# A feed-forward stage after attention: kept weights, inputs fetched during attention, VectorE's work in other pieces, and opening maxima in three buffers

## The reference

```python
x = x + 0.5 * ffn(layernorm(x), Wr, We)
x = x + attention(layernorm(x), Wq, bq, Wk, bk, Wv, bv, Wo, bo)   # 16 heads of 16, rotary q and k
x = x + 0.5 * ffn(layernorm(x), Wr, We)

def ffn(x, Wr, We):                      # 8 experts, each 256x256; both FFNs have the same weights
    logits = x @ Wr.T
    top_vals, top_idx = top_k(logits, 2); w = softmax(top_vals)
    # token t goes to its two experts if fewer than C = 1537 earlier picks of its sequence went there
    out[t] = sum over k of w[t, k] * (x[t] @ We[top_idx[t, k]]) if kept
```

## Time and profile before

| | us |
|---|---|
| median of 3 runs | 6634.64 (6630.81 to 6637.87) |
| profiled execution, its own time | 6634.04 |
| its span (profile) | 6632.2 |
| TensorE busy | 6263.3 (94%) |
| VectorE busy | 6035.8 (91%) |
| ScalarE busy | 4754.6 (72%) |
| GpSimd busy | 379.1 (6%) |

### The profile page before, as it was taken

One profiled execution on the slowest core, in us unless ns is written; L12 is line 12 of the kernel. 1 busy time (PEld: TensorE's weight loads), 2 busy tenths in 40 slices (PEclk: granted clock), 3 DMA queues, 4 the chain that ended last, 5 costly groups with the idle time before them and its releaser, 6 DMA issues. The chain is left out here.

```text
span 6632.2 us, 158232 instructions
## 1 busy us (share of the span) xinstructions
PE 6263.3 (94%) x54288; PEld 2797.8 (42%) x54288; DVE 6035.8 (91%) x6991; ACT 4754.6 (72%) x8698; POOL 379.1 (6%) x604
## 2 busy tenths in 40 slices
PE   7888579999999999999999999999999999996888
PEld 6666423333333333333333333333333333334666
DVE  7888579999999999999999999999999999963766
ACT  2222128888888888888888888888888888882111
POOL 2322300000000000000000000000000000001221
PEclk9999769999999999999999999999999999997999
DMA  2222301010100101010101010101010100001110
GB/s 80 93 91 94 89 10 16 13 16 13 16 17 13 19 10 19 10 19 10 19 10 23 10 22 14 16 13 16 13 16 13 17 16 13 3 3 66 42 47 25
DMA packets 120611, 177.08 MB, mean 27 GB/s; under 512 B 61616, under 2 KB 78784, under 8 KB 116800
## 3 DMA queue, kind: packets, MB, share of 16 engines
q1 hardware_dynamic: 120128, 169.43, 11.0%
HBM read 100.17 MB, written 69.21 MB: 26 GB/s over the span
## 5 line engine op out<-in xcount | busy, mean ns | idle before, releaser
L972 DVE TENSOR_REDUCE at_mx<-at_m 128x1 f32<-128x1024 f32 x4096 | 5008.5, 1224 | 117.3 <-PE at_m L849 97.0
L948 ACT ACTIVATE at_ex<-at_s 128x512 f32<-128x512 f32 x8192 | 4450.2, 595 | 754.9 <-PE at_s L870 185.7
L849 PE MATMUL at_m<-at_k,at_q 48*128 48x512 f32 x8192 | 3005.2, 449 | 63.4 <-DVE at_mx L972 50.0
L870 PE MATMUL at_s<-at_q,at_k 50*128 50x512 f32 x8192 | 2996.9, 444 | 0.0
L880 PE MATMUL at_po<-at_ex,at_v 128*32 128x256 f32 x32816 | 2624.5, 392 | 31.7 <-POOL at_v L818 31.7
L849 PEld LDWEIGHTS at_m<-at_k,at_q 48*128 48x128 f32 x8192 | 1214.7, 187 | 1769.5 <-DVE at_mx L972 1692.4
L880 PEld LDWEIGHTS at_po<-at_ex,at_v 128*32 128x32 f32 x32816 | 646.5, 108 | 1519.8 <-issue 748.1
L870 PEld LDWEIGHTS at_s<-at_q,at_k 50*128 50x128 f32 x8192 | 1211.8, 185 | 42.6 <-ACT at_ex L948 42.2
L272 PE MATMUL fr_ps<-fr_weh,fr_xl 128*128 128x512 f32 x512 | 179.5, 433 | 108.6 <-DVE fr_acc L443 108.6
L824 POOL COPY at_v<-at_vst 128x1024 f32<-128x1024 f32 x16 | 16.7, 1043 | 4598.1 <-DMA at_vst<-v_by_head 4283.5
L1202 PE MATMUL bk_ps<-bk_weh,bk_xl 128*128 128x512 f32 x512 | 172.3, 418 | 64.9 <-DVE bk_acc L1328 64.8
(11 more groups left out here) (167 smaller groups left out, 2664.9 us busy)
## 6 DMA issues: line engine op xcount, KB each, us to landing
at_q<-q_parts SPq DMA_DIRECT2D x96, 256.0 KB, 5.0
at_k<-k_parts SPq DMA_DIRECT2D x96, 256.0 KB, 6.3
q_parts<-fr_parts SPq DMA_DIRECT2D x64, 256.0 KB, 2.2
k_parts<-fr_parts SPq DMA_DIRECT2D x64, 256.0 KB, 2.4
attended<-at_o SPq DMA_DIRECT2D x256, 34.0 KB
fr_x<-in_x SPq DMA_DIRECT2D x16, 512.0 KB, 4.3
after_ffn<-fr_acc SPq DMA_DIRECT2D x16, 512.0 KB, 3.0
v_by_head<-fr_v SPq DMA_DIRECT2D x16, 512.0 KB, 4.1
```

Of the source, the lines that this page charges most:

```text
L849: ins = pe.matmul(pm[w][:, h * QB:(h + 1) * QB], Q[p][rows, base + i * P:base + (i + 1) * P], K[p][rows, c * CW + h * QB:c * CW + (h + 1) ...
L870: pe.matmul(ps[event(t) % NS][:, :], K[p][rows, j * P:(j + 1) * P], Q[p][rows, sb_ * QU + g * QB:sb_ * QU + (g + 1) * QB], start=True, sto ...
L948: ac.activation(Ex[QUAD * (j % NX) + 2 * g + 1 - half][:, :], ps[event(t) % NS][:, :], ACT.Exp)\
L972: ve.tensor_reduce(out=mx[u][:, i, c:c + 1], in_=pm[w][:, :], op=ALU.max, axis=AX.X)\
```

## The change

- Weights, their split parts and the constants of both FFNs (ident, wr, before, ones, order, weh, wel) are allocated around all three phases and made once, by front_phase. back_phase has no loads or splits of them.
- New tiles and semaphores (ahead_tiles) live through attention and back_phase. SyncE fills them in the last head pair: at its first unit the sums of sequence 0, three constants and the inputs of groups 0 and 1 (fetch_ahead), at its last unit the reciprocals (fetch_reciprocals_ahead). VectorE takes those of sequence 0 at the end of its work in attend_phase. The sums of sequence 1 are loaded at the start of back_phase and inverted in group 0.
- The opening maxima use three buffers (pm[0], pm[1] and two of the three banks of the scores), a whole chunk after the other. VectorE's first two units stand outside its loop, for the buffers' names.
- In back_phase the orders of TensorE and VectorE are others, at the start and in each group, and product 15 goes to bank 1.

```diff
-        ps = [ctx.enter_context(nc.psum_tensor(f"{name}_s{k}", [P, QB], F32)) for k in range(NS)]
+        s_all = ctx.enter_context(nc.psum_tensor(f"{name}_s", [P, NS * QB], F32))
+        ps = [s_all[:, k * QB:(k + 1) * QB] for k in range(NS)]
+        first = [pm[0], pm[1], s_all[:, 0:CW]]
+        FIRST = 2 * (STEPS + AHEAD)
...
+                        if not more and sb_ == 0:
+                            hold(sp, s_out, (2 + PB * SB) * (QUAD * DMA), s_tick)
+                            fetch(sp)
+                        if not more and sb_ == SB - 1:
+                            fetch_reciprocals(sp)
                         hold(sp, s_e, u * EVENTS + (EVENTS + COPY_AT + 1 + E0), s_tick)
...
+                def first_chunk(n):
+                    m, w = n // 2 % STEPS, n % 2
+                    i, c, base = m // CQ, m % CQ, n // RED * QU
+                    if n >= len(first):
+                        pe.wait_ge(s_mr, 2 + n - len(first) + 1)
+                    rows = slice(HALF * w, HALF * w + ROWS)
+                    for h in range(2):
+                        last = pe.matmul(first[n % len(first)][:, h * QB:(h + 1) * QB],
+                                         Q[0][rows, base + i * P:base + (i + 1) * P],
+                                         K[0][rows, c * CW + h * QB:c * CW + (h + 1) * QB], start=True, stop=True)
+                    last.then_inc(s_m, 1)
...
-                for m in range(STEPS + AHEAD):
-                    for half in (0, 2, 1, 3):
-                        max_chunk(m % STEPS, half, 0, m // STEPS * QU, m // STEPS)
+                for n in range(FIRST):
+                    first_chunk(n)
...
+                ve.wait_ge(ahead.s_sum, GB * DMA)
+                ve.reciprocal(ahead.recs[0][:, :], ahead.sums[0][:, :]).then_inc(ahead.s_all, 1)
...
+def fetch_ahead(sp, t, sources, constants):
+    attended, residual, _, sums, _ = sources
+    for src, dst in sums(t.sums[0], 0):                 # 8 pieces
+        sp.dma_start(dst, src).then_inc(t.s_sum, DMA)
+    for dst, src in zip((t.spread[:, :], t.wo[:, :, :], t.bo[:, :]), constants):
+        sp.dma_start(dst, src).then_inc(t.s_c, DMA)
+    for u in range(2):
+        for c in range(NC):
+            sp.dma_start(t.at[u][:, c, :], attended(u, c)).then_inc(t.s_at[u], DMA)
+        sp.dma_start(t.x[u][:, :, :], residual(u)).then_inc(t.s_x[u], DMA)
+
+def fetch_reciprocals_ahead(sp, t, sources, tick):
+    _, _, reciprocals, _, store = sources
+    hold(sp, t.s_all, 1, tick)
+    for dst, src in store(t.recs[0], 0):                # 8 pieces
+        sp.dma_start(dst, src).then_inc(t.s_rd, DMA)
+    hold(sp, t.s_rd, GB * DMA, tick)
+    for u in range(2):
+        sp.dma_start(t.rec[u][:, :], reciprocals(u)).then_inc(t.s_rec[u], DMA)
...
+    BANK = [n % NB for n in range(CHUNKS - 1)] + [1]
...
-                        if n == 0:
-                            need(pe, s_ac, g * STEPS)
+                        if n < 2:
+                            need(pe, s_ac, g * STEPS - (0 if n else EP * NB))
                         elif n >= NB:
-                            pe.wait_ge(s_ac, g * STEPS + EP * (n - NB + 1))
+                            last_use = max(m for m in range(n) if BANK[m] == BANK[n])
+                            pe.wait_ge(s_ac, g * STEPS + EP * (last_use + 1))
...
-                pe.wait_ge(s_c, 7 * DMA)
-                for n in range(2):
-                    spread_out(n, n, 0)
-                    project(n)
+                pe.wait_ge(s_c, 3 * DMA)
+                spread_out(0, 0, 0)
+                project(0)
                 turn(0)
+                spread_out(1, 1, 0)
                 router(0)
-                pe.wait_ge(s_wl, 1)
+                project(1)
                 positions(0)
```

More of the change, by code:

```diff
@@ L103, in sem @@
             return nc.alloc_semaphore(f"{name}_{n}")
[L105 to L108, removed]
+        ident, wr, before, ones, order, weh, wel = shared
+        before32, keep = sb("before32", [P, P]), sb("keep", [P, NG])
         pq_in, pv_in = sb("wqk", [P, NC, 4, P]), sb("wv", [P, NC, D])
@@ L1008, in _, with back_sources, attended, residual @@
                     split(n, NPAIR * SB)
-def back_phase(nc, name, x1, att, rec_dram, weights, biases, consts, out):
-    We, Wo, Wr = weights
-    ident_in, spread_in, before_in, order_in = consts
+                ve.wait_ge(ahead.s_sum, GB * DMA)
+                ve.reciprocal(ahead.recs[0][:, :], ahead.sums[0][:, :]).then_inc(ahead.s_all, 1)
+def back_sources(x1, att, rec_dram):
+    rows = att[0:HD, :, :, :].rearrange("d h b s -> (d h) b s").rearrange("(c p) b s -> p c b s", p=P)
+    sums = att[HD:HD + 1, :, :, :].rearrange("o h b s -> (o h) b s")
+    def attended(g, c):
+        return rows[:, c, :, :].rearrange("p b s -> p (b s)")[:, bass.ds(g * GT, GT)]
+    def residual(g):
+        return x1[bass.ds(g, 1), :, :, :].rearrange("g p i d -> p (g i) d")
+    def reciprocals(g):
+        return rec_dram.rearrange("h b s -> h (b s)")[:, bass.ds(g * GT, GT)]
+    def pieces(dram, tile, b):
+        return [(dram[:, b:b + 1, k * GT:(k + 1) * GT].rearrange("h b s -> h (b s)"), tile[k * H:(k + 1) * H, :])
+                for k in range(GB)]
+    return attended, residual, reciprocals, lambda tile, b: pieces(sums, tile, b), lambda tile, b: pieces(rec_dram, tile, b)
+def fetch_ahead(sp, t, sources, constants):
[14 more added lines that the diff above has]
+    hold(sp, t.s_rd, GB * DMA, tick)
+    for u in range(2):
+        sp.dma_start(t.rec[u][:, :], reciprocals(u)).then_inc(t.s_rec[u], DMA)
+def back_phase(nc, name, shared, ahead, sources, out):
+    attended, residual, reciprocals, sums_of, recs_of = sources
     EP = 2
@@ L1030, in sem @@
             return nc.alloc_semaphore(f"{name}_{n}")
[L1032 to L1041, removed]
+        ident, wr, before, ones, order, weh, wel = shared
+        at, rec, xg, wo, bo_sb, spread, sums, recs, s_at, s_rec, s_x, s_c, s_sum, s_all, s_rd = ahead
+        keep = sb("keep", [P, NG])
         an = sb("an", [P, NC, GT])
-        xg = [sb(f"x{u}", [P, TG, D]) for u in range(2)]
         xb = sb("xb", [P, TG, D])
@@ L1139, in body @@
                         load_residual(g + 4, u)
+                    if isinstance(g, int) and g == 1:
+                        hold(sp, s_all, 2, s_tick)
+                        for dst, src in recs_of(recs[1], 1):
+                            sp.dma_start(dst, src).then_inc(s_rd, DMA)
+                        hold(sp, s_rd, 2 * GB * DMA, s_tick)
                     hold(sp, s_ac, g * STEPS + STEPS, s_tick)
@@ L1314, in normal, with combine @@
                     last.then_inc(s_xn, 1)
-                def combine(g, u, it, i):
-                    if i == 0:
+                def combine(g, u, it, i, first=0, end=E):
+                    if i == 0 and first == 0:
                         need(ve, s_wt, g + 1)
                         need(ve, s_st[u], it * DMA)
-                    for e in range(E):
+                    for e in range(first, end):
                         n = i * E + e
```

153 lines of the change are left out of this document (79 added, 74 removed).

## The result

The changed kernel took 6544.1 us (median of 4 runs, 6538.67 to 6548.38) beside 6636.2 for the one before (4 runs, 6630.81 to 6637.87): ratio 0.9862, 95% interval 0.9845 to 0.9879. The profiled execution took 6538.67, its span 6536.8; before it was 6632.2, so 95.4 less.

What follows compares the result with a forecast made beforehand. ScalarE's exponentials fill attention, untouched; the gains lie in stretches beside it where no engine is full. Opening 37, start 31 and groups 23 sum to 91 us, giving 6544 us; range 6518 to 6572, about 0.84.

Steps and rivals of the forecast that it cites:

- The opening: Maxima before attention: three buffers let VectorE set the pace at 1.13 us a chunk; gain 37 us, between 31 and 38.
- The round trip: Opening: SyncE's trip of the found maxima ends at 893.5, before the first score at 899.9, so stays hidden by 6 us.
- The clock in unit 0: Attention's first unit: a denser opening might raise TensorE's clock earlier, saving up to 8 us; counted as nothing.
- The start: Attention's end to the second FFN's first expert product: loads, splits and reciprocals leave the chain; gain 31 us, bounds 29 and 33.5.
- What was moved: Last head pair: SyncE's 8 us of loads fit in 14 us free; of VectorE's other half of reciprocals 1 us shows.
- The groups: Second FFN's groups: new order cuts waits, 34.2 to 32.8 us each, 17 us, plus 6 of low clock; 23, bounds 5 and 45.
- The walk's waits: Steady second-FFN group, stepped through in the new order: TensorE idles 1.4 us before the transposes and 1.5 before product 15.
- The low clock stays: Rival, chance 0.15: second FFN's two 1.5 us gaps a group hold TensorE's clock down as often as before; 6550 us.
- The groups gain nothing: Rival, chance 0.12: VectorE in smaller pieces is late for two products, second FFN's group period stays 34.9; 6567 us.
- TensorE is the bound: Rival, chance 0.08: second FFN's groups have no stall and no low clock, 30.5 us a group; 6503 us.
- the opening stays tied: Rival, chance 0.04: opening maxima keep 1.62 us a chunk, through slow TensorE or the round trip coming last; 6581 us.
- Slower, by attention's exponentials: Rival, chance 0.03: with tiles moved in SBUF, attention's exponentials come every 0.627 us instead of 0.614, costing 107 us; 6651 us.

Runs made afterwards that it cites:

- e1: The kernel before the change, with only the opening changed to three buffers in whole-chunk order; median 6608.3 us, ratio 0.9945, opening 91.62 us.
- e2: The changed kernel with two buffers in the opening instead of three, whole-chunk order kept; 6553.7 us, ratio 0.9866, opening 101.4 us.
- e3: The changed kernel with the second FFN's groups in the old order on TensorE and VectorE, old bank and waits; 6565.2 us, ratio 0.9890.
- e8: The changed kernel with VectorE's norm and its choice of experts for the next group both moved earlier; 6488.4 us, ratio 0.9780.
- e12: e8 with the 64-byte tile of kept counts moved behind the expert inputs, without an unused tile; 6478.5 us, ratio 0.9756.
- e11: e10 with the 64-byte tile of kept counts moved behind the expert inputs; 6480.5 us, ratio 0.9761.
- e10: e8 with an unused tile of 16960 bytes a partition ahead of the kept expert weights; 6488.6 us, ratio 0.9773.
- e4: The changed kernel with inputs, sums and reciprocals fetched at the second FFN's start, weights still kept on chip; 6556.2 us, ratio 0.9869.
- e5: The changed kernel with product 15 back in bank 0, so product 0 waits for the whole previous group; 6558.0 us, ratio 0.9885.
- e7: The changed kernel with VectorE's choice of the next group's experts put between the halves of combine 2; 6516.6 us, ratio 0.9817.
- e9: The changed kernel with an unused tile of 16960 bytes a partition ahead of the kept expert weights; 6544.2 us, ratio 0.9856.

## Why the prediction was right

The sum was 91 us. The median fell by 92.1, the profiled span by 95.4.

- **The opening, 37.** Measured 38.1, and e1 shows it alone. The higher of the two bounds was right, as the pairs in the same rows said: maxima in a row come 1.13 apart, though one of them is shown with 1.22. The walk from first maximum to first score gave 90.45 and took 90.4. The round trip stayed hidden. TensorE's side of it was too light (0.85 for a latency of 1.22), which made no difference with three buffers; with two, in e2, it is why a chunk costs 1.26.
- **The clock in unit 0, taken at 0 with 8 kept for the range.** After the first score the low level lasted 10.6 us, until 914.5, instead of 17.1, and attention gained 2.8. It is not the change's: in twelve profiles with that same opening the low level lasted 10.6 to 34.4 us, in four of them 17.1 to 17.3 as before, and the first interval was 79.6 to 89.9.
- **The start, 31 (29 to 33.5).** Measured 34.3, outside the bounds. The mechanism is right and two terms were too large: TensorE started 0.2 us after SyncE's first issue, where I took the middle between SyncE and GpSimd, 1.8 late; from TensorE's start to the first product it was 29.0 instead of 30.3, mostly since the first projection took 5.61 and not 6.55.
- **What was moved.** 14 us of free time on SyncE for 8 us of loads: right, nothing was late. VectorE's reciprocals in attention cost no unit anything. Of the other half the prediction says that 1 us shows, and leaves it out of its sum; the first group, which has them, took 33.1 us, no more than the others.
- **The groups, 23 as 17 of waits and 6 of clock.** Measured 24.5. The walk's waits of 1.4 and 1.5 are 1.33 and 1.60. Its period of 32.8 is 33.3; up to 0.45 of the difference is the matmuls' new spacing (96 of them, 4.7 ns each), which I had excluded. From before to after, the first group (from its first expert product to that of the next group) gave 4.8 us, its clock 0.88 becoming 1.00; the next eleven gave 18.8, and the last four 0.9. Of the 18.8, some 6 are three groups that had clock 0.95 and now 1.00. So the waits gave about 1.1 a group and not 1.4. e3 has the old order at the new spacing: its groups at clock 1.00 take 34.4 to 35.1 us, 34.7 on average, and beside them the order and the bank are worth the walk's 1.4. So the mechanism is right. That the sum of 23 met 24.5 is in part luck: the waits gave less than 17 (and 13 groups at 1.4 are 18, not the 19 of the prediction), and the clock gave more than 6, of which e1 shows that it varies from one execution to the next.
- **The low clock stays (0.15).** It didn't: two groups at 0.95 or less, the thirteenth and the fifteenth, where the kernel before had six. In eleven groups in a row the two waits of 1.33 and 1.60 left the clock at 1.00; the gaps beside its two falls were 3.28 and 4.67. The first FFN of the same execution shows the other side, where TensorE has gaps of 2.3 to 3.0 us in every group, two neighbouring windows:

```profile
374.31:418.37 44.06, 35.37 (x182) 28.43 (x181) 38.33 (x95) 11.27 (x19) 13.13 (x18) 1.00 0.28 91
418.37:466.46 48.09, 39.74 (x182) 31.82 (x181) 38.24 (x98) 12.21 (x20) 13.32 (x19) 0.89 0.27 91
```

  In the later groups of that phase the clock falls in every second one, at 4 us each time. The Trainium skill (TensorE: Matmul & The Clock Gate, A second HAM failure mode) says that frequent small idles between groups of matmuls made the clock oscillate in a kernel that it measured. This trace agrees for the first FFN, with its three gaps in every 44 us. It doesn't for the steady groups of the second, where two shorter gaps in every 33 us did it nowhere.
- **The groups gain nothing, TensorE is the bound, the opening stays tied.** None came true. TensorE's bound is 29.96 us a group at this spacing, as e8 shows, not 30.5; the changed kernel stops 3.3 short of it for two orders of VectorE's work.
- **Slower, by attention's exponentials.** They kept their pace, 79.0 us a unit (the prediction's 79.2 is 129 times 0.614). But the sentence against it, that no row shows an operation depending on where its tile lies, was true of the rows and wrong of the chip: e12 moves tiles by 64 bytes and the expert products' spacing changes by 2%.

## What to carry to other kernels

Where two engines hand buffers to each other, take the time that a buffer needs to go round, latency of the products included, and divide by the number of buffers: the longer of that and the slower engine's own pace is the time of a chunk, and here it came out within 0.1 us. Walk a group once with each engine's order written out; each wait that remains names the piece of work to move, and here two such moves gave another 53 us, a part of it by the clock. In comparing single executions, compare stages, and keep apart those that hold a clock change.

## What the runs showed of the hardware

- Matmuls of 128x512 with four-byte operands started 228.5 or 233.3 ns apart at 2.4 GHz, depending on a shift of the input tiles by 64 bytes. With weights (the moving operand, 512 columns) 89600 bytes a partition ahead of the inputs (the stationary one, 128 columns) it was 228.6 (before, e1, e11, e12, at two absolute places); with 89664 it was 233.3 (after and e2 to e10, at two places). Tiles between them (attention's normed values, residuals, norms) moved along by the same 64 bytes, so that the distance is the cause is an inference from four layouts. The first FFN bears on it: by the sizes of the tiles ahead, its inputs lie 76832 bytes behind the weights in before and e1 and 77408 in the others, and the same products start 233.3 and 232.6 to 232.9 ns apart there, with other work beside them. Of these four distances only 89600 is a multiple of 128; whether that is what counts was not tried.
- With the same opening, the clock rose 10.6 us after the first score in the changed kernel and 34.4 us after it in e10: the first interval was 79.6 in the one and 89.9 us in the other, and 82.5 and 84.3 occurred too. TensorE was marked busy without a gap all that time. What decides it stays open.
- VectorE's pause in the norm of the changed kernel's thirteenth group, 1.98 us with no releaser in the trace, stood at that place in e2 (1.86), e4 (1.81), e5 (1.84), e7 (2.02) and e9 (2.07) too. In e8 there is none in the norm; VectorE idles 2.69 us there ahead of a combine, which the trace puts down to TensorE. The thirteenth group is the first behind the loop; what the pause is stays open.
